# Scatters of a mixture-of-experts layer: four semaphores in turn and at most four transfers in flight

## The reference

```
x      = layernorm(x).reshape(1600, 256)
logits = x @ router_w                        # 8 experts, top 2, capacity 500
combine, dispatch = top2_gating(logits, 500)
expert_in  = einsum('nec,nh->ech', dispatch, x)
hmid       = silu(expert_in @ w1 + b1)       # 1024 wide
expert_out = hmid @ w2 + b2
y      = einsum('nec,ech->nh', combine, expert_out)
shared = silu(x @ sw1 + sb1) @ sw2 + sb2
out    = y + 0.1 * shared
```

## Time and profile before

| what | us |
|---|---|
| median of three runs | 1088.35 |
| lowest and highest of them | 1081.34, 1095.97 |
| the profiled execution's own time | 1081.66 |
| its span, first to last instruction | 1079.6 |

### The profile page before, as it was taken

One profiled execution on the slowest core, in us unless ns is written; L12 is line 12 of the kernel. 1 busy time (PEld: TensorE's weight loads), 2 busy tenths in 40 slices (PEclk: granted clock), 3 DMA queues, 4 the chain that ended last, 5 costly groups with the idle time before them and its releaser, 6 DMA issues.

```text
span 1079.6 us, 22058 instructions
## 1 busy us (share of the span) xinstructions
PE 829.0 (77%) x7910; PEld 615.3 (57%) x7910; DVE 707.0 (65%) x1454; ACT 552.8 (51%) x1210; POOL 264.7 (25%) x264
## 2 busy tenths in 40 slices
PE   3657787777788754873988999997655898787995
PEld 2335565555565533551775767775213676646995
DVE  7646666666677547840658667753698657586766
ACT  3425555565565412640427555554897546383542
POOL 2235334334344100556000000001642000062300
PEclk9668989999999856795999999998556879698998
DMA  6553444444444534642226655644210000010001
GB/s 162 107 125 102 123 118 124 123 119 124 124 111 116 145 129 169 199 127 71 79 79 194 176 155 159 204 124 123 72 48 9 1 1 0 26 52 1 3 1 61
DMA packets 80009, 107.62 MB, mean 100 GB/s; under 512 B 21075, under 2 KB 62093, under 8 KB 79862
## 3 DMA queue, kind: packets, MB, share of 16 engines
q1 hardware_dynamic: 73346, 97.86, 32.4%
q0 software_dynamic: 4096, 6.57, 2.1%
q10 hardware_dynamic: 2500, 2.31, 0.7%
HBM read 85.58 MB, written 20.92 MB: 99 GB/s over the span
## 4 chain that ended last, share of the span: by engine, by line
PE 35%; DMA 26%; DVE 11%; SPq 10%; issue 9%; ACT 6%; POOL 2%; another core or an unknown queue 1%; ACTq 0%; DVEq 0%; POOLq 0%
PE ps L1102 10%; DMA k_parts<-kp 9%; PE ps L1089 8%; DMA floor<-floor_q 7%; DMA den<-o 4%; PE ps L1608 3%; SPq L2469 2%; PE ps L2052 2%; PE ps L1602 2%; DMA pick_more<-in_L_ffn_sb_dram 2%; ACT area L1564 1%; PE ps L1597 1%; PE ps L2063 1%; SPq L434 1%; SPq L438 1%
## 5 line engine op out<-in xcount | busy, mean ns | idle before, releaser
L532 DVE TENSOR_REDUCE m<-ps 100x2 f32<-100x722 f32 x128 | 114.5, 898 | 64.4 <-PE ps L527 64.4
L1151 ACT ACTIVATE hT<-ps,cols 128x500 f32<-128x500 f32 (+1 forms) x96 | 62.5, 651 | 127.1 <-PE ps L1089 93.3
L567 DVE SCALAR_TENSOR_TENSOR p<-p,xe 121x600 f32<-121x600 f32 x128 | 102.4, 802 | 20.4 <-DMA xe<-floor 20.4
L552 ACT ACTIVATE p<-ps 121x600 f32<-121x600 f32 x128 | 85.5, 668 | 50.4 <-PE ps L545 48.6
L1158 DVE TENSOR_TENSOR hT_l<-hT,hT_h 128x500 f16<-128x500 f32 (+1 forms) x96 | 62.3, 652 | 73.9 <-ACT hT_h L1152 60.9
L1102 PE MATMUL ps<-w_h,hT_h 128*125 128x256 f16 (+1 forms) x384 | 105.5, 275 | 1.8 <-DVE x L1197 1.2
L1102 PE MATMUL ps<-w_l,hT_h 128*125 128x256 f16 (+1 forms) x384 | 105.4, 275 | 0.0
L1102 PE MATMUL ps<-w_h,hT_l 128*125 128x256 f16 (+1 forms) x384 | 105.4, 274 | 0.0
L1089 PE MATMUL ps<-xe_h,w_h 128*128 128x500 f16 (+1 forms) x192 | 72.0, 375 | 25.6 <-issue 12.1
L1445 POOL PARTITION_ALL_REDUCE gmax<-cmax x6 | 2.2, 366 | 358.7 <-DVE cmax L1440 352.7
L527 PE MATMUL ps<-ks,qs 128*100 128x361 f16 x256 | 66.2, 346 | 28.1 <-DMA qs<-q_parts 26.5
(11 more groups left out here) (329 smaller groups left out, 2123.8 us busy)
## 6 DMA issues: line engine op xcount, KB each, us to landing
xe<-floor SPq DMA_DIRECT2D x32, 378.1 KB
sw<-in_L_ffn_w_dram SPq DMA_DIRECT2D x16, 512.0 KB, 7.2
sw<-in_L_ffn_w_dram SPq DMA_DIRECT2D x8, 1024.0 KB, 5.7
stage<-in_L_xattn_W_f_dram SPq DMA_DIRECT2D x6, 1024.0 KB, 8.5
k_parts<-kp SPq DMA_DIRECT2D x32, 181.5 KB, 4.0
ks<-k_parts SPq DMA_DIRECT2D x32, 181.5 KB
ctx_f<-in_ctxT_dram SPq DMA_DIRECT2D x16, 270.8 KB, 4.3
stage<-in_ctxT_dram SPq DMA_DIRECT2D x8, 541.5 KB, 8.5
```

Of the source, the lines that this page charges most:

```text
L532: v.tensor_reduce(m32[p][:, 2 * i:2 * i + 2], ps[0:T, at:at + 2, 0:KV], AX.X, ALU.max).then_inc(m_max, 1)
L552: s.activation(p32[:, i % HALF, :, :, :].rearrange("p j n t -> p n j t"), ps[0:KT, t_bank(i):t_bank(i) + 2, 0:KJ * T].rearrange("p n (j t) ...
L567: v.scalar_tensor_tensor(probs, probs, 1.0, low, ALU.min, ALU.max).then_inc(a_cv, 1)
L1151: s.activation(hT[:, f % 3, 0:m], bank[2 + f % 2][:, 0:m], ACT.Silu, bias=bias, scale=1.0 / WS)
```

## The change

The semaphore `scat` goes. The scatters, numbered m = 16 n + b, increment `got[0]` to `got[3]` in turn, and each from the fifth on first waits until the one four places earlier has landed. After the scatters each of the four stands at 16 * 32 / 4 = 128 (`SCAT`), for which ScalarE waits before it loads the first slots, and the gathers later count on from there: VectorE waits for 64 + 128 on the first four and for 64 on the others. What is computed and the order of all other instructions stay as they were; line numbers shift by one to four.

```diff
-        scat = sem("scat")
...
-        got = [sem(f"got{n}") for n in range(B // 2)]
+        FLIGHT = 4
+        SCAT = 16 * 2 * B // FLIGHT
+        got = [sem(f"scat_got{n}" if n < FLIGHT else f"got{n}") for n in range(B // 2)]
...
             if is_shared(n) and n == NG - 2:
-                s.wait_ge(scat, 16 * 2 * B)
+                for m in range(FLIGHT):
+                    s.wait_ge(got[m], SCAT)
                 for e in range(2):
                     expert_slots(s, e, e)
...
-                v.wait_ge(got[i // 2], 64)
+                v.wait_ge(got[i // 2], 64 + (SCAT if i // 2 < FLIGHT else 0))
...
             for n in range(2):
                 g.wait_ge(r_idx, n + 1)
                 for b in range(B):
+                    m = n * B + b
+                    wait(g, got[m % FLIGHT], 16 * (m // FLIGHT))
                     g.indirect_dma_start(xs_d, bass.IndirectOffsetOnAxis(ap=into[n][:, b:b + 1], axis=0),
-                                         xn[:, b, :], None).then_inc(scat, 16)
+                                         xn[:, b, :], None).then_inc(got[m % FLIGHT], 16)
```

## The result

| | before | after |
|---|---|---|
| median | 1086.36 us (4 runs, 1081.34 to 1095.97) | 1075.97 us (4 runs, 1072.98 to 1079.54) |
| ratio, 95% interval | | 0.9898 [0.9856, 0.9940] |
| profiled execution, span | 1081.66, 1079.6 us | 1079.54, 1077.4 us |

The change gains about 1%, inside the 2% that was called no change. Both profiled executions lie at one end of their runs, so they differ by less than the medians do.

What follows compares the result with a forecast made beforehand. It took TensorE to be the bound, with a 31.3 us hole during the scatters that would stay; cap 0.4 plus waits 0.5 us add 0.9 us at most, so 1088 us against a median of 1088.35, range 1052 to 1104.

Steps and rivals of the forecast that it cites:

- no change: Whole kernel: a time within about 2% (22 us) of before, which a measurement cannot tell apart; chance 0.57.
- The cap would bind once at most: GpSimd's scatters: the cap may hold only scatter 5, during the early jam, for 0.4 us, between 0 and 1.3.
- 28 wait instructions: On GpSimd, between scatters: 17 ns each, 0.5 us in all, at most 8.4 us, at least 0 or slightly below.
- The sum: GpSimd's scattering grows by 0.4 us for the cap plus 0.5 us for the wait instructions, 0.9 us.
- The semaphores in turn are free: ScalarE's load of the first slots waits on four counts instead of one, with 36 us of cover: no cost.
- TensorE's increment was seen 14.2 us late: During the scatters: TensorE's count earned at 477.71 us was seen by VectorE's L1197 only at 491.93 us.
- The hole stays: TensorE's near-idle stretch during the scatters, 478.0 to 514.6 us, remains with the cap idle; chance 0.57, 1079 to 1100 us.
- The signs that the prediction named: Scatters 1.3 us apart, 42 us in all; TensorE hole of 20 to 40 us; waits of 10 us before L1151, L1197.
- The hole costs 31.3 us: TensorE, 478.0 to 514.6 us: 36.6 us spent on 37 matmuls worth about 5.3 us, so 31.3 us lost.
- The cap binds: Rival: late scatter completions make GpSimd wait at each scatter and keep the hole open; about 1112 us, chance 0.14.
- if the hole lasts as long as the scattering, all of it is on the path: GpSimd's scattering: its 0.9 us growth adds fully to the kernel's time in that case, otherwise nothing.
- The first rival: Spread semaphores and a look back at completions cure TensorE's hole: 1057 us, or 1067 if a third stays; chance 0.29.

Runs made afterwards that it cites:

- cap_eight: The changed kernel with eight semaphores and a cap of eight instead of four, so 24 waits, none of which lasts; ratio to before 1.0012.
- cap_one: The changed kernel with a cap of one: each scatter waits until the one before it has landed; 1106.85 us, ratio to before 1.0183.
- drain_four: The kernel before, with a wait ahead of every fourth scatter until all scatters given out so far have landed; 1062.90 us, ratio 0.9787.
- cap_two: The changed kernel with a cap of two scatters in flight instead of four; 1068.34 us, ratio to before 0.9795.
- eight_bursts: The kernel before, scatters in eight bursts of four, each set to wait for a later hidden block of TensorE's; 1058.63 us, ratio 0.9729.
- no_scatters: The kernel before without its 32 scatters and without ScalarE's wait for them; 1051.39 us, ratio 0.9673.
- gathers_there: The changed kernel with a cap of eight, its 32 scatters replaced by 32 gathers from HBM into SBUF; 1082.37 us, ratio to before 0.9963.
- one_wait: The changed kernel with only one wait between scatters, before the sixth for the second to have landed; 1080.61 us, ratio to before 0.9926.

## Why the prediction was right

**Point by point.**
- *The cap would bind once at most, ahead of scatter 5, for 0.4 us, between 0 and 1.3.* It bound once, for 1.17 - 0.30 = 0.87 us, within those bounds and at the place named: the prediction counts from 0 (m = 5, which needs m = 1), so its scatter 5 is the sixth of the timeline.
- *28 wait instructions cost 0.5 us, between 0 and 8.4.* They cost nothing: the 0.30 us gap between two scatters is unchanged, and `cap_eight` with 24 of them is 1.0012 [0.9981, 1.0043]. They fall into the gap, the lower bound. The sum, 0.9 us, came out as measured (42.4 against 41.5) because the two errors cancel.
- *The semaphores in turn are free.* Yes: 0.9993 without the cap.
- *TensorE's increment was seen 14.2 us late.* VectorE was at other work until 480.13 us, so only the 11.8 us of its idling are shown. Nothing in the sum hangs on the difference.
- *The hole stays.* Yes: 24.5 us of it, in place of 30.9. The signs that the prediction named are there: scatters 1.3 us apart, 42 us in all, waits of 10 us and more put down to "remote" before L1152 and L1198, though "issue" before these lines is now in smaller pieces.
- *The hole costs 31.3 us, and its going would bring 1057 us.* By landmarks 30.9 us, and the kernel without scatters takes 1051.39 us, 34.4 below before in the same group. The stretch had been read right; the base was the median of three runs, 1088.35, and the medians of larger sets were 1086 to 1092.
- *The cap binds, 1112 us.* It did not. The quantity L that this rival hung on, the time until a scatter's landing is seen, is 2.6 to 2.7 us in the last 17 scatters of `cap_one`, well under the 5.2 us from which a cap of four holds; beside SyncE's loads two earlier ones passed that. The Trainium skill (Perfetto Trace Analysis, section "DMA Instruction — HWDGE (DVE, Sync)") speaks of a surprisingly long final update with HBM as target. For these scatters the trace shows 2.66 us from start to landing, so it is not long here. The mechanism is real all the same: with a cap of one it costs 52.8 us in T, 1106.85 us, near the 1112 that was said for a binding cap, and by another road, namely ScalarE's late load and not the hole.

**What was missed.** The forecast's step "if the hole lasts as long as the scattering, all of it is on the path" took the pause for a pure cost: 0.9 us or nothing. By this mechanism the sign was wrong, and "no change" held only because the gain stayed under the 22 us allowed for noise, which is luck. It was a gain of 10 us (1086.36 - 1075.97; of these S shows 30.9 - 24.5 = 6.4 us between the two profiled executions, and the one of before is itself 4.7 us under its median). The first rival had named the cure ("given out without ever looking back") but expected that it needs a pile for the cap to clear, and counted either the whole hole or a third of it left. What works is a pause in the giving out: one of 0.9 us moves TensorE's stop from 11 to 20 us after the first scatter, pauses after every fourth scatter or about every second (`drain_four`, `cap_two`) remove the hole to within 1 us, and in `eight_bursts` two early ones of 6.0 and 1.1 us left 3.8 us.

**How the sum closes.** The profiled execution of `no_scatters` took 1052.69 us. With the losses of the table the others should take: before 1083.6 (1081.66 measured), after 1077.2 (1079.54), `cap_eight` 1089.1 (1088.47), `cap_two` 1063.8 (1065.96), `drain_four` 1063.9 (1063.67), `cap_one` 1105.5 (1106.16), `gathers_there` 1080.8 (1081.74). Two don't close, `one_wait` (1077.9 against 1083.42) and `eight_bursts` (1056.5 against 1067.28); they lost time in other stages. That the rest closes to about 2 us is in part chance, since the stages ahead of S vary too: S begins at 471.69 us in before and at 476.46 in after. Nor do the profiles show the whole 10 us between the medians, only 6.4 to 6.8 us of it in S.

**What stays open.** Why a stream of scatters makes a hole at one place and not at another, and why rests help. The wake-ups that come late sometimes end at a rest of GpSimd's or just behind its last scatter, but some end in mid-stream (VectorE at 491.93 us in before), so there is no simple rule "held until the next rest". It was not tried whether a rest that GpSimd spends on other work serves as well, nor what a single rest does at another place. Whether TensorE's increments leave late or the others see them late can't be told from these views.

One rival was not tested: that the engines run out of instructions, whose loads the profile lists among the same transfers as the scatters. The traces speak partly against it. The queue "q8 instruction" moves one load for every 125 to 143 matmuls in `no_scatters`. In before one load comes at 465.6 us and the next at 515.5, behind the hole, and 142 matmuls lie between them, against 141 in `no_scatters`: if that queue is TensorE's, its loads came on time for the work it did. But in after such a load falls at 491.7 us, just where TensorE begins to crawl, and nothing here tells whether that is chance.

## What to carry to other kernels

- A GpSimd queue full of row-wise transfers, given out back to back, can hold up the other engines although nothing in the program makes them wait; it need not. Look for "issue" and "remote" waits of 10 us and more on TensorE, VectorE or ScalarE beside it, price it by leaving the transfers out once (34 us here), and put pauses into the stream; here those in its first third did most.
- Check in the trace that a wait put in to make a pause does make one. Of the seven later waits of `eight_bursts` two held. It was the fastest kernel all the same: 3.8 us lost in S, and its last scatter was out in time.
- A cap on transfers in flight is a way to make rests, and its size is a trade. Reckon with period = landing time / cap as the least (2.7 us here, so a cap of four never holds in the steady part; a cap of two gave 1.99 us, not 1.35), and check when the last transfer is needed: what the rests lengthen must end before that, or the gain comes back as a late load.

## What the runs showed of the hardware that was not expected

While GpSimd gives out 32 indirect transfers of 100 rows each, 1.3 us apart, the shared layer loses 31 to 36 us out of 41.5, and 28 us when gathers take their place. It is not only waking up late: inside one group of matmuls without a semaphore between them TensorE pauses mostly for 0.8 to 2.2 us after every one to four (the chain of after above). With one in flight and a transfer every 3.4 us on average the loss is 0.0 us, and in a later part of the same layer 20 transfers in an unbroken stream, 1.6 us apart on average, cost nothing (`eight_bursts`). The Trainium skill (SBUF — State Buffer, section "SBUF: two separate sides") says that of the engines only VectorE and GpSimd can block one another in SBUF, and that TensorE and ScalarE never wait on anyone. The pauses within TensorE's group are therefore nothing that this rule foresees; that they are SBUF's doing is not shown, and if the rule holds they come from somewhere else.
